# First pass of a four-layer channel-mixing kernel: 32-column quarters of TensorE's array, a shared column of ones, sums added on GpSimd, strips fetched later

## The reference

```python
# for each of the 15 partitions of {i0, i1, o0, o1}
out += einsum(..., X, W[k]) / denom      # X, X^T, diagonal, row sum, column sum, trace, total
# the block around it, four times: normalise, convolve, add to the stream
m = mean(x); v = var(x); (x - m) / sqrt(v + 1e-5)
```

## Time and profile before

| | |
|---|---|
| median of 3 executions | 2340.03 us |
| the profiled execution, its own time | 2337.63 us |
| its span, first to last instruction | 2335.7 us |
| mean granted TensorE clock | 0.979 of full speed |
| TensorE busy | 1993.8 us, 85% |
| VectorE busy | 1366.4 us, 58% |
| DMA | 835.82 MB, 358 GB/s on average |

### The profile page before, as it was taken

One profiled execution on the slowest core, in us unless ns is written; L12 is line 12 of the kernel. 1 busy time (PEld: TensorE's weight loads), 2 busy tenths in 40 slices (PEclk: granted clock), 3 DMA queues, 4 the chain that ended last, 5 costly groups with the idle time before them and its releaser, 6 DMA issues.

```text
span 2335.7 us, 25806 instructions
## 1 busy us (share of the span) xinstructions
PE 1993.8 (85%) x11026; PEld 1395.5 (60%) x11026; DVE 1366.4 (58%) x1559; ACT 28.9 (1%) x76; POOL 66.0 (3%) x98
## 2 busy tenths in 40 slices
PE   8999999999999999969987777777777777777775
PEld 8999999999999999953332222222222222222221
DVE  7666667667666666533665555555555555555554
ACT  0000000000000000000000000000000000000000
POOL 4000000000000000100000000000000000000000
PEclk9999999999999999967999999999999999999998
DMA  9888888888888898612999999999999999999999
GB/s 336 321 318 317 320 319 307 316 320 325 312 319 316 305 321 302 224 36 108 372 427 427 427 427 426 428 427 427 427 426 427 426 428 427 427 427 427 427 427 386
DMA packets 115882, 835.82 MB, mean 358 GB/s; under 512 B 14712, under 2 KB 14840, under 8 KB 15416
## 3 DMA queue, kind: packets, MB, share of 16 engines
q1 hardware_dynamic: 78632, 565.06, 63.0%
q10 hardware_dynamic: 37136, 269.11, 27.3%
HBM read 564.73 MB, written 269.09 MB: 357 GB/s over the span
## 4 chain that ended last, share of the span: by engine, by line
PE 51%; DMA 46%; DVE 3%; issue 0%; ACT 0%; SPq 0%; DVEq 0%
PE ps L625 42%; DMA ring_own<-strip_in 25%; DMA out<-ring_own 20%; PE ps L704 6%; DVE ring_own L586 1%; DVE ring_own L594 0%; PE ps L684 0%; PE ps L686 0%; PE ps L680 0%; DMA const<-const_f 0%; PE ps L640 0%; PE ps L634 0%; PE ps L711 0%; PE ps L611 0%; PE ps L710 0%
## 5 line engine op out<-in xcount | busy, mean ns | idle before, releaser
L625 PE MATMUL ps<-early 128*128 128x132 f32 x8704 | 979.6, 276 | 0.3 <-ACT dia_cov L399 0.3
L625 PEld LDWEIGHTS ps<-early 128*128 128x128 f32 x8704 | 979.4, 190 | 0.5 <-ACT dia_cov L399 0.5
L462 DVE TENSOR_REDUCE part_sum<-early 128x32 f32<-128x2048 f32 x272 | 621.8, 2286 | 315.5 <-DMA early<-pairs 313.8
L704 PE MATMUL ps<-ring_own,mixer 128*128 128x512 f32 x1380 | 632.5, 603 | 190.0 <-DMA ring_own<-strip_in 190.0
L704 PEld LDWEIGHTS ps<-ring_own,mixer 128*128 128x128 f32 x1380 | 250.9, 191 | 572.9 <-issue 568.5
L586 DVE SCALAR_TENSOR_TENSOR ring_own<-ps,row_term,col_term 128x1536 f32<-128x1536 f32 (+3 forms) x259 | 332.8, 1285 | 380.7 <-PE ps L704 380.7
L704 PE MATMUL ps<-early,mixer 128*128 128x512 f32 x672 | 307.1, 601 | 98.8 <-DMA early<-strip_in 98.8
L704 PEld LDWEIGHTS ps<-early,mixer 128*128 128x128 f32 x672 | 121.2, 189 | 284.6 <-issue 283.1
L586 DVE SCALAR_TENSOR_TENSOR early<-ps,row_term,col_term 128x1024 f32<-128x1024 f32 (+1 forms) x126 | 161.4, 1281 | 182.1 <-PE ps L704 182.1
L594 DVE SCALAR_TENSOR_TENSOR ring_own<-ps,row_term,col_term 128x508 f32<-128x508 f32 (+56 forms) x340 | 147.3, 475 | 0.0
L594 DVE SCALAR_TENSOR_TENSOR early<-ps,row_term,col_term 128x468 f32<-128x468 f32 (+55 forms) x168 | 72.8, 475 | 0.0
(11 more groups left out here) (140 smaller groups left out, 154.4 us busy)
## 6 DMA issues: line engine op xcount, KB each, us to landing
early<-pairs SPq DMA_DIRECT2D x272, 1056.0 KB, 5.2
ring_own<-strip_in SPq DMA_DIRECT2D x172, 1024.0 KB, 45.4
out<-ring_own ACTq DMA_DIRECT2D x172, 1024.0 KB, 36.4
early<-strip_in SPq DMA_DIRECT2D x84, 1024.0 KB, 45.4
out<-early ACTq DMA_DIRECT2D x84, 1024.0 KB, 36.5
const<-const_f SPq DMA_DIRECT2D x1, 778.0 KB, 7.2
dia<-dia_pair SPq DMA_DIRECT2D x1, 640.0 KB, 3.7
ring_own<-strip_in SPq DMA_DIRECT2D x1, 512.0 KB, 6.2
```

What stands on the lines that cost most here:

```text
L462: nc.vector.tensor_reduce(part_sum[:, t % 2], vbuf[:, s].rearrange("p (k w) -> p k w", w=CW)[:, :, 0:BLK].rearrange("p k (c a) -> p c k a" ...
L625: last = mm(ps[:, (r % 2) * MARK + m, 0:CW], vbuf[:, s, k * CW:k * CW + BLK], vbuf[:, s, k * CW:(k + 1) * CW], start=opens and k % MARK == ...
L704: last = mm(ps[:, first + at // BANK, 0:piece], mixer[:, :, :].rearrange("p c a -> p (c a)"), zbuf[s][:, at:at + piece], start=True, stop= ...
```

## The change

It does six things.

- A tile's 64 rows become 64 chunks of one row. A chunk has 32 numbers a partition, so its weights are 32 columns wide. Chunk `k` uses the 32-column quarter `k % 4` of the array, by way of the PSUM partitions that its output stands on. Two neighbouring chunks share one column of ones that lies between them: the even chunk streams its 32 numbers and the one behind them, the odd chunk the one ahead and its 32 numbers. A partition of a tile is 2080 numbers long instead of 2112.
- `col_sum` is added up by GpSimd, behind a ring of 20 `part_sum` buffers instead of 2; VectorE keeps only the reduction, now over a pattern that reads every number 32 or 33 places behind the last.
- There are 4 tile slots instead of 6, and 17 slots in `ring_own` instead of 12. Several buffers are laid into others (`f1s`, `coef_s` and `col_term` into `stage`; `wt`, `dia2`, `dia2s` and `brow` into the last slots of `ring_own`).
- No strip is fetched during the first pass: all 17 own slots are filled behind the last tile, then 3 of the 4 that come from `early`.
- The constants and the diagonal are fetched behind the fourth tile; the product over the diagonal moves to the opening of range 2.
- The row sums leave PSUM in four ScalarE copies a range, one a quarter, instead of one.

```diff
-CHUNKS = RANGE // SUB
-MARK = 4
-CW = BLK + MARK
+WROWS = 1
+WIDE = PAIR * WROWS
+COLS = BLK // WIDE
+CHUNKS = RANGE // WROWS
+REGIONS = CHUNKS // COLS
+BANK_REGIONS = 4
+SUMS = 20
+TWO = 2 * WIDE + 1
+VW = CHUNKS // 2 * TWO
-V_SLOTS = 6
+V_SLOTS = 4
...
-        Z_OWN = 12
+        Z_OWN = 17
...
-        reuse = max(0, after - -(-mid_at[0] // n))
+        reuse = after - 1
...
+        def regions(r):
+            half = ps[:, r % 2 * 4:r % 2 * 4 + 4, 0:BANK_REGIONS * (WIDE + 2)]
+            return half.rearrange("p b (m w) -> p b m w", m=BANK_REGIONS)
+
+        def by_channel(s):
+            slot = vbuf[:, s]
+            return bass.AP(slot.tensor, slot.offset, [list(slot.ap[0]), [WROWS, PAIR], [TWO, CHUNKS // 2],
+                                                      [WIDE + 1, 2], [1, WROWS]])
...
-                if t % gap == gap - 1 and fetched < min(Z_OWN, len(order)):
-                    if fetched == Z_OWN - place_slots:
-                        sp.wait_ge(matrices_in, 16 * 13)
-                    load_strip(fetched)
-                    fetched += 1
+                    sp.dma_start(const[:, :], const_f32).then_inc(const_in, 16)
+                    sp.dma_start(dia2[:, :, :], dia_pair).then_inc(dia_loaded, 16)
+                    sp.dma_start(dia_in[:, :, :], dia).then_inc(dia_loaded, 16)
...
+            own_slots = min(Z_OWN, len(order))
+            for p in range(own_slots):
+                if p == Z_OWN - early_slots:
+                    sp.wait_ge(matrices_in, 16 * 13)
+                    sp.wait_ge(dia_cov_done, 1)
+                load_strip(p)
...
-            for r in range(nr):
-                pool.wait_ge(gram_staged, r + 1)
-                if r:
-                    pool.wait_ge(gram_added, r)
-                nc.gpsimd.tensor_tensor(gram4[:, :, :], gram4[:, :, :], stage[:, r % 2], ALU.add).then_inc(gram_added, 1)
+            for t, (r, J) in enumerate(tiles):
+                pool.wait_ge(summed, t + 1)
+                if t:
+                    pool.wait_ge(sum_added, t)
+                nc.gpsimd.tensor_tensor(col_sum[:, J], col_sum[:, J], part_sum[:, t % SUMS], ALU.add).then_inc(sum_added, 1)
+                if last_of_range[r] == t and r:
+                    add_gram(r - 1)
+            add_gram(nr - 1)
...
-                if t >= 2:
-                    dve.wait_ge(sum_added, t - 1)
+                if t >= SUMS:
+                    dve.wait_ge(sum_added, t - SUMS + 1)
+                nc.vector.tensor_reduce(part_sum[:, t % SUMS], by_channel(s), AX.XYZ, ALU.add).then_inc(summed, 1)
...
-            pe.wait_ge(dia_scaled, 1)
-            for b in range(nb):
-                last = mm(ps[0:FEATS, 0, 0:FEATS], dia2s[:, b], dia2[:, b], start=b == 0, stop=b == nb - 1)
-            last.then_inc(dia_multiplied, 1)
-            pe.wait_ge(dia_cov_done, 1)
...
+                if opens and r == 2:
+                    pe.wait_ge(dia_scaled, 1)
+                    for b in range(nb):
+                        last = mm(dia_acc, dia2s[:, b], dia2[:, b], start=b == 0, stop=b == nb - 1)
+                    last.then_inc(dia_multiplied, 1)
+                    pe.wait_ge(dia_cov_done, 1)
...
                 for k in range(CHUNKS):
-                    m = k // MARK
-                    last = mm(ps[:, (r % 2) * MARK + m, 0:CW], vbuf[:, s, k * CW:k * CW + BLK],
-                              vbuf[:, s, k * CW:(k + 1) * CW],
-                              start=opens and k % MARK == 0, stop=closes and k % MARK == MARK - 1)
+                    m, lane, odd = k // COLS, k % COLS * WIDE, k % 2
+                    at = k // 2 * TWO + odd * (WIDE + 1)
+                    last = mm(regions(r)[lane:lane + WIDE, m // BANK_REGIONS, m % BANK_REGIONS, 1 - odd:WIDE + 2 - odd],
+                              vbuf[:, s, at:at + WIDE], vbuf[:, s, at - odd:at - odd + WIDE + 1],
+                              start=opens and m % BANK_REGIONS == 0, stop=closes and m % BANK_REGIONS == BANK_REGIONS - 1)
                 last.then_inc(gram_done, 1)
```

More of the change, by code:

```diff
@@ L66, in lay_out @@
                 z[q, h, :, :, at:at + width] = a[:, SUB * g:SUB * g + SUB, j:j + width]
[L67 removed]
+    return v.reshape(len(tiles), BLK, VW), z.reshape(len(strips(n)), BLK, n)
 def put_back(strip_out, diag_out, n):
@@ L98, in gram_place @@
         m = np.zeros((BLK, FEATS))
-        m[:, first:first + CH] = own_chan * weight[:, None] / (2. * n * n)
+        m[:, first:first + CH] = (v_chan[:, None] == np.arange(CH)) * weight[:, None] / (2. * n * n)
         return m
@@ L268, in load_strip @@
                 sp.dma_start(zbuf[s][:, 0:width], z[q, :, 0:width]).then_inc(z_in[s], 16)
-            fetched = 0
-            gap = max(1, len(tiles) // (Z_OWN + 2))
             for t in range(len(tiles)):
```

147 lines of the change are left out of this document (73 added, 74 removed).

## The result

The changed kernel takes 2429.9 us, the median of four executions (2426.0 to 2432.2), against 2339.8 (2338.3 to 2341.8, four executions) of the kernel before on the same chip: a ratio of 1.0383 with a 95% interval of 1.0365 to 1.0401. It is 90 us slower; the forecast was 2224, 116 us faster. The profiled execution took 2425.97 us.

A forecast was written before the change was run, and what follows sets the result against it. TensorE was taken to bound the first pass, DMA the second. 2337.6 - 98.4 (first pass) - 17.2 (second pass) = 2222.0, with the median 2.4 higher 2224 us; forecast's own range 2170 to 2260, whole range 2018 to 2470 (0.82).

The forecast's parts named there:

- the time of a tile: First pass: 3.25 us a tile, quarters overlapping but held by 256 instructions being fetched and issued; chance 0.34.
- the 26 ns step: TensorE: shortest distance between two matmuls in the earlier trace, at the slow clock; 128 of them make 3.33 us a tile.
- the forecast's formula: Whole time from c us a tile in the first pass: 2340.0 + 272c + 12.5 - 994.9 - 17.2.
- Rival 1: First pass: DMA alone bounds, quarters overlap fully, 2.51 to 2.6 us a tile, 2023 to 2048 us; chance 0.24.
- Rival 2: First pass: quarters do not overlap or only in part, 3.7 to 4.16 us a tile, 2350 to 2472 us; chance 0.26.
- the break-even: First pass: nothing is gained at 3.68 us a tile, or 28.7 ns a pair.
- Rival 3: First pass: issue bounds, each instruction of a pair needs 26 ns, 6.66 us a tile, 3152 us; chance 0.12.
- Rival 4: First pass: VectorE's reduction slows with scattered reading, at twice the time 4.57 us a tile, 2584 us; chance 0.04.
- the stall of 7 us: Start of the first pass: TensorE is done with four tiles at 18.5 us, the fifth lands near 25.5.
- the second pass: After the layers: 7 full strips fewer to read, 17.2 us less, lasting about 1238 us.
- a granted clock below full: Sign in the profile's first pass: it would say that TensorE waits much.
- TensorE and VectorE both waiting for tiles: Sign in the first pass that instructions hold one DMA engine, with the DMA share below 0.9.

The follow-up runs named there:

- e11: e2 with only the first four tiles fetched and used over and over for the whole first pass: 2368.1 us.
- e10: e5 with six tile slots and 15 own strip slots instead of 4 and 17: 2106.1 us, ratio 0.9009.
- e5: The changed kernel with two rows a chunk: 32 chunks of 64 columns in two halves of the array, 128 instructions a tile: 2108.2 us, ratio 0.9003.
- e3: The changed kernel with the chunks reordered so that 16 in a row use the same quarter of the array: 2546.6 us.
- e2: The changed kernel with only the pattern of VectorE's reduction put back to runs of four: 2426.9 us.
- e14: e5 with only the first four tiles fetched and used over and over: 1985.3 us.
- e8: e5 with 32 small matmuls of 33 columns by 1 added to each tile, so 256 instructions again: 2607.7 us.

## Why the prediction was wrong

**The step that failed** is the time of a tile, "I take 3.25 us a tile ... the quarters overlap, yet a tile is held by 256 instructions being fetched and issued". The words were right and the mechanism behind the number was not: 4.00 us. I priced a block of 256 instructions by what its packet takes on one engine, 0.61 to 0.86 us beside the tile's share, so that the tile would land late, and otherwise by the 26 ns step of the earlier trace rows. Neither is what happened. The packet does take only 0.95 us, but no tile was late: TensorE waited 7.2 us for tiles in the whole pass and 543.7 us in "issue". It can't go on until the next packet has come, and that is a round of its own. In the changed kernel's records a packet begins 1.60 us after TensorE has resumed, takes 0.95, and TensorE resumes 1.38 us after its end: 3.93, against 4.02 from one resumption to the next. Before, a packet was needed every 4 tiles, 14 us apart, and the round lay hidden; with one-row chunks it is needed every tile, of which TensorE works 1.98 us. By the forecast's formula, c = 4.00 gives 2340.0 + 1088.0 + 12.5 - 994.9 - 17.2 = 2428; measured were 2430.

The start of the packet moves with the traffic of the tiles: 1.13 us after the resumption without traffic (e11), 1.60 at a DMA share of 0.78, 3.07 at 0.98 (e10), 3.6 (three packets) when the strips were queued behind the last tiles of the changed kernel. There the same 128 pairs are followed by twice the idle time. Timeline of TensorE, changed kernel, the pass's end:

```profile
1075.43 1.99 PE L644 MATMUL ps<-early 128*32 128x33 f32 x128 [1.64 <-issue]
1081.65 1.98 PE L644 MATMUL ps<-early 128*32 128x33 f32 x127 [4.22 <-issue]
1087.74 1.99 PE L644 MATMUL ps<-early 128*32 128x33 f32 x128 [4.11 <-issue]
```

The Trainium skill, *Runtime: NRT & Kernel Launch*, section Instruction fetch mechanics, has the same block of 256 instructions and says that its cost is mostly hidden because engines issue more slowly than the blocks arrive. The trace agrees on the block and disagrees on the hiding: at 56 ns an instruction (half of the 112.5 of the earlier trace rows) TensorE stayed behind its fetch, at 7.8 ns (1.99 us / 256) it outran it.

**Rival 1** (transfers alone bound, 2023 to 2048) didn't come: DMA share 0.78, not 1.0. Without the instruction round there was room for it; e5 came within 60 us of its upper edge.

**Rival 2** has the time (2350 to 2472) and the sign, and its mechanism is refuted: e3 is what not overlapping looks like, 2547 us, and the changed kernel's pairs are twice as fast at half the clock. L711 and L710 were, as I wrote, a weak witness; what sets them apart is not settled. So the break-even that I gave, 28.7 ns a pair, was crossed (31.3 ns on average), but by 13.7 ns of work and the rest standing. That the time lies in this rival's range is chance.

**Rival 3** (issue bounds, 3152) is refuted as it was put: no single instruction is slow, they go at 7.8 ns each while a block is there. What it had right is that TensorE stands while nothing else is late.

**Rival 4** (VectorE slows with scattered reading) is true as a mechanism, 3782 ns and not the 2286 that I expected to stay, because the earlier trace rows only held runs of four. I had put the price at twice (4.57) and it is 1.65 times. It costs nothing here (e2), by 0.22 us a tile; had the fetch been faster, it would have been the next bound, at 2340 + 272 x 3.8 + 12.5 - 994.9 - 17.2 = 2374 us. So the forecast of 2224 was out of reach for a second reason.

**Right:** 291 instruction packets (about 290); GpSimd's add at 251 ns (bounded by 310) under an idle engine; the first matmul at 5.8 us (5.5 was forecast, although the terms given for it, 0.75 + 5.2, make 5.95); the stall of 7 us behind the first tiles (7.2 us of waiting for tiles in the pass); the layers unchanged (+0.7); the strips hidden in the layers, the second pass 12.5 us shorter (17.2 worked out). **Right as a sign:** a granted clock below full, given as the mark of much waiting. It costs nothing by itself, since the work of 1.98 us ends inside the round (4.00 us from block to block at full clock, too). **Wrong as a sign:** the forecast wanted TensorE and VectorE both waiting for tiles with the DMA share below 0.9. The share was 0.78, but they waited 7.2 and 66.6 us for tiles in a pass of 1089.

**Without a row before:** that TensorE stops for instructions at all. The kernel before has 0.3 us of idle time in the line. What it could have told is how far the forecast reached: in the first pass a packet had lasted 14 us, and one packet each 3.25 us was four times that rate, with no row that said what a packet costs from its request on. That unknown was priced from below only.

That e3 stops as well, 195 times and 156.6 us in all, fits the same round: its 128 pairs last 3.7 us, and its packets begin 1.83 us after the first record of the block ahead and take 0.94, so with the 1.4 us behind them the next block comes after 4.2.

**Left open:** why the next packet begins only 1.1 us after the resumption with nothing else on the queues, and not at once, and what fills the 1.4 us from its end to the first instruction; why e3's stops are longer in every second block. Nor is it shown whether an arrangement between two and three tiles in flight would beat 2106 us.

## What to carry to other kernels

Count the instructions between two units of work before making matmuls smaller. On TensorE 256 of them (64 f32 matmuls) needed about 3.75 us to arrive with DMA idle, 4.0 at 0.78 of DMA and 5.7 to 6.1 when the queues are full; work that is shorter than this per 256 instructions gained nothing from being made shorter. The array's quarters do overlap, so tile the array, but only as far as the instructions allow: two rows a chunk gave 10%, one row lost 4%.

The mark in a profile is an idle time "issue" of 1 to 4 us behind every 128 matmul records, with the granted clock at 0.5 and nobody late.

## What the runs showed of the hardware

- A block of 256 TensorE instructions, one 16 KB packet, comes every 3.74 us at best (e11), 4.02 in the changed kernel, 5.66 at a DMA share of 0.98 (e10), 6.09 with strips queued at 423 GB/s. It is fetched one block ahead: the packet begins at the earliest about when the block before it does (within 2 us in the kernel before, 0.31 us behind it in e14).
- f32 matmuls of 33 columns in the four quarters begin 6 to 7 ns apart if neighbours differ in quarter, four per 55 ns at 1.2 GHz, a pair each 8.8 ns at 2.4 GHz; in one quarter a pair takes 29 ns at 2.4 GHz. The Trainium skill, *TensorE: Matmul & The Clock Gate*, section "Wait — 56ns, not 53.3ns?", says that starts never come closer than about 25 ns, and the rule that the prediction cited from *TensorEngine Tiling (Array Packing)* has the same floor; across quarters the trace disagrees with both.
- VectorE sums 2048 f32 numbers a partition in 2286 ns if each is next to the last or comes in runs of four or more, 2400 in runs of two, 3566 to 3809 if none has its neighbour read next, at distances from 4 to 33.
- TensorE busy 99 of 200 us was granted 0.50, busy 150 of 200 (e5) 0.97, busy 174 of 200 (e8, 500 to 700 us) 0.83: the busy share alone does not tell the clock.
